# A scan of sixteen steps moved two slots later in a software pipeline of two layers on one core

## The reference, cut to what matters

```python
xn = layernorm(x)                                          # layer 0
s  = (q @ k.T * GAMMA ** (i - j)) @ v                      # retention
h  = silu(tlin(xn, w1)) * tlin(xn, w2)                     # "z"
h  = gelu(tlin(h, h1)); h = gelu(tlin(h, h2))
x  = x + s * silu(tlin(h, w3))
xn = layernorm(x)                                          # layer 1
x_ssm, gate = split(xn @ W_in + b_in)
xc = silu(causal_conv(x_ssm, 4 taps) + conv_b)
B, C = split(xc @ W_x + b_x)
h_t = exp(-exp(A_log)) * h_(t-1) + xc_t[:, None] * B_t     # 128 features x 16 states
y_t = sum over states of C_t * h_t, + D * xc_t
s  = (y * silu(gate)) @ W_out + b_out
x  = x + s * silu(router_ffn(xn))                          # top 512 of 1024 tokens by score
```

## Time and profile before

| what | us |
|---|---|
| median of 3 runs | 546.79 (545.92 to 547.64) |
| the profiled execution | 545.56 |
| its span, first to last instruction | 543.8 |
| busy: PE, DVE, POOL, ACT | 443.4, 407.9, 404.7, 291.4 |

### The profile page before, as it was taken

How to read it: one execution, slowest core, us unless ns; L and a number is a source line. 1 busy time by engine, 2 the same in 40 slices (tenths; PEclk the granted TensorE clock), 3 DMA queues, 4 the chain that set the end, 5 groups by cost and what they waited for, 6 DMA issues and landing times.

```text
span 543.8 us, 6040 instructions
## 1 busy us (share of the span) xinstructions
PE 443.4 (82%) x1777; PEld 259.0 (48%) x1791; DVE 407.9 (75%) x659; ACT 291.4 (54%) x475; POOL 404.7 (74%) x316
## 2 busy tenths in 40 slices
PE   0796978898889897989899888989798999485743
PEld 0575645644564455545565456445554464131211
DVE  2282144959788977989598959898789779958985
ACT  3664736774567545763676366745676447313300
POOL 1673543887599959985999769985999599855582
PEclk9997979899999999999999999999999999978865
DMA  8300006311513143221532162214321332215220
GB/s 316 136 20 4 1 0 175 85 51 40 155 60 86 50 125 108 77 77 47 152 96 78 37 176 77 79 39 118 115 79 58 96 99 78 78 44 165 85 74 19
DMA packets 25379, 46.97 MB, mean 86 GB/s; under 512 B 3072, under 2 KB 4096, under 8 KB 25088
## 3 DMA queue, kind: packets, MB, share of 16 engines
q1 hardware_dynamic: 24336, 45.13, 28.1%
q10 hardware_dynamic: 1008, 1.41, 0.8%
HBM read 42.33 MB, written 4.19 MB: 86 GB/s over the span
## 4 chain that ended last, share of the span: by engine, by line
POOL 35%; DVE 23%; issue 17%; PE 16%; ACT 5%; DMA 1%; SPq 0%; DVEq 0%; POOLq 0%; ACTq 0%
POOL hs L548 15%; DVE hs L1359 10%; PE bank0a L932 7%; DVE xbank L1336 7%; POOL hidAl L510 6%; POOL hidBl L510 5%; PE bank1a L1012 2%; POOL xnTl L492 2%; POOL g L526 2%; POOL g L522 2%; DMA Bt<-w_in 1%; POOL xr L530 1%; POOL q L499 1%; PE ybank L1071 1%; DVE st L1262 1%
## 5 line engine op out<-in xcount | busy, mean ns | idle before, releaser
L548 POOL TENSOR_TENSOR hs<-hs,Ct 128x512 f32<-128x512 f32 x127 | 184.6, 1459 | 32.6 <-DVE hs L1359 19.7
L510 POOL TENSOR_TENSOR hidAl<-plain,hidAh 128x512 fp32r<-128x512 f32 x48 | 64.6, 1346 | 37.7 <-ACT hidAh L643 31.3
L1359 DVE TENSOR_TENSOR_SCAN hs<-decay,carry,xbank 128x512 f32<-128x512 f32 x63 | 80.5, 1278 | 7.6
L510 POOL TENSOR_TENSOR hidBl<-plain,hidBh 128x512 fp32r<-128x512 f32 x48 | 66.1, 1378 | 26.6 <-ACT hidBh L643 18.7
L1359 DVE TENSOR_TENSOR_SCAN hs<-decay,xbank 128x512 f32<-128x512 f32 x64 | 78.0, 1219 | 5.6 <-DVE xbank L1336 0.5
L1336 DVE TENSOR_TENSOR xbank<-xs,bbank 128x512 f32<-128x512 f32 x104 | 71.4, 687 | 1.3
L642 ACT ACTIVATE plain<-bank0a,col 128x512 f32<-128x512 f32 x64 | 44.2, 690 | 45.2 <-PE bank0a L932 44.0
L932 PE MATMUL bank0a<-hidBh,hTh 128*128 128x512 f32 x128 | 57.7, 451 | 1.7 <-ACT q L675 1.7
L932 PE MATMUL bank0a<-hidAh,hTh 128*128 128x512 f32 x128 | 57.0, 445 | 1.7 <-ACT q L675 1.7
L932 PE MATMUL bank0a<-hidAl,hTh 128*128 128x512 f32 x128 | 51.6, 403 | 0.0
L932 PE MATMUL bank0a<-hidBl,hTh 128*128 128x512 f32 x128 | 50.7, 396 | 0.0
(11 more groups left out here) (184 smaller groups left out, 951.7 us busy)
## 6 DMA issues: line engine op xcount, KB each, us to landing
xs<-x_rows SPq DMA_DIRECT2D x128, 256.0 KB, 3.4
xt<-x_tok SPq DMA_DIRECT2D x8, 256.0 KB, 4.5
xr<-x_feat SPq DMA_DIRECT2D x8, 256.0 KB, 7.6
x_rows<-xc SPq DMA_DIRECT2D x8, 256.0 KB, 2.0
out<-xr SPq DMA_DIRECT2D x7, 256.0 KB, 2.2
fh<-h_w SPq DMA_DIRECT2D x1, 1024.0 KB, 10.0
hs<-h_w SPq DMA_DIRECT2D x1, 1024.0 KB, 11.9
lw<-l_w ACTq DMA_DIRECT2D x1, 640.0 KB, 5.4
```

The costliest lines, as they stand in the source:

```text
L510: pool.tensor_tensor(low[:, m, :], plain[:, k % NPLAIN, :], high[:, m, :].bitcast(F32), ALU.subtract).then_inc(hidden_low, 1)
L548: pool.tensor_tensor(h, h, Ct[:, hs_(u)], ALU.mult).then_inc(p_ready, 1)
L1359: dve.tensor_tensor_scan(hs[:, i % NSTATES, :], decay[:, gr:gr + 1].broadcast_to([P, HALF]), xbank[:], 0.0 if u % 2 == 0 else carry[:, k:k ...
```

## The change

`LEAD` goes from 8 to 10: slots 10 to 15 hold steps 0 to 5, and slots 0 to 9 of the next period hold steps 6 to 15. All that belongs to the scan moves with it: DVE's two instructions and POOL's `weigh_states` of each step by two slots, quads 1, 2 and 3 from slots 1, 4, 8 to 3, 6, 10, quad 0 only from 14 to 15, `gate_y` from 9 to 12, ACT's copy of B from 8 to 11. SP's row transfers no longer come as four at once in slot 6; they follow one per slot across the units. The last period has two slots more.

```diff
-LEAD = NGRP // 2
+LEAD = 10
...
-                if n is not None and s == 6:
+                if n == 0 and s == 6:
                     for k in range(NROWS - 1):
-                        spread_x(n, k)
+                        spread_x(0, k)
                 u, k = scanned(p, s)
-                if u is not None and k + NROWS - 1 < NGRP:
-                    spread_x(u, k + NROWS - 1)
+                if u is not None and step(u, k + NROWS - 1) <= LAST:
+                    spread_x(*divmod(step(u, k + NROWS - 1), NGRP))
...
                     elif s == 8:
                         score_columns(n)
-                        keep_B(n)
...
+                if n is not None and s == 11:
+                    keep_B(n)
...
-                    if s in (1, 4) and t is not None:
-                        gather_y(t, 1 if s == 1 else 2)
+                    if s in (3, 6) and t is not None:
+                        gather_y(t, 1 if s == 3 else 2)
...
-                    if s == 8 and t is not None:
+                    if s == 10 and t is not None:
                         gather_y(t, 3)
...
-                    if t == UNITS - 1 and s == 9:
+                    if t == UNITS - 1 and s == 11:
                         project_last()
...
-                    if n is not None and s == 14:
+                    if n is not None and s == 15:
                         gather_y(n, 0)
...
-                    if t == UNITS - 1 and s == 8:
+                    if t == UNITS - 1 and s == 10:
                         finish_last()
-                    elif t < UNITS - 1 and s == 9:
+                    elif t < UNITS - 1 and s == 12:
                         gate_y(t)
```

## The result

| | before | after |
|---|---|---|
| median, us | 546.95 (545.92 to 547.64, 4 runs) | 586.37 (583.48 to 589.67, 4 runs) |
| ratio | | 1.072 (1.066 to 1.079) |
| span of the profiled execution, us | 543.8 | 587.9 |
| mean granted clock | 0.95 | 0.90 |

The change makes the kernel 7.2% slower. The forecast had the sign and half of the size: 20 us where the medians show 39.4. The profiled execution after is the slowest of its four (589.67 us), so what is read from it adds up to 44.1 us of span.

A forecast was written before the change was run, and what follows sets the result against it. POOL's list was taken to bound stretch B (from zero, POOL's first low part of h1 in slot 6, to DVE's residual), a chain through DVE stretch A; 18.0 for six periods + 0.5 + 1.1 = 19.6, giving 567 us, range 552 to 580.

The forecast's parts named there:

- DVE's holes: DVE's idle waits for the new B and the gate's product, 41.8 us; filling them was claimed to give 0.
- SP's queue and B's copy: Row transfers one per slot and ACT's 0.6 us copy in slot 11; claimed value 0 for both.
- Quad 3, slot 8 to slot 10: PE's quad ahead of h2 waits for POOL's step of slot 9; h2 3.3 us later a period, ends 1.7 and 3.8.
- the 3.8 of the upper end: h2's start 3.8 us later, if POOL pays its whole stall before the step of slot 9 instead of beside it.
- The 0.5 that I took off for `rstd`: POOL's 1.02 us `rstd` may run beside the wide comparison in every other period; h2's delay 3.3 instead of 3.8.
- clock mostly kept: Part of the main forecast, chance 0.44: PE waits in slot 10, 3 us a period, its clock mostly not falling.
- the rival given 0.26: PE's clock falls in most periods around the slot 10 wait, 1.8 us more a period, 577 us; chance 0.26.
- Quad 0: Slot 14 to 15, behind `mod_up`, ahead of `ffn_out`: silu starts 0.5 us later a period, slack used up.
- -0.8 for quads 1 and 2: Quad 2 leaves the chain ahead of the convolution, -1.00; quad 1 costs about 0.2; -0.8 a period, ends -1.0 and 0.
- Start and end: Period 0 gets only quad 0's +0.5; the end +4.4 for two more steps, -2.2 and -1.1 for waits, +1.1.
- the signs that the prediction named: Quad 3 waits 2 us or more, h2 some 17 after zero, POOL idle, residual waits 3 or more, period 61 to 63.

The follow-up runs named there:

- experiment 4: Kernel after plus 4 + 2 PE products that nobody reads, ahead of and behind xn's transposes in slot 9; 567.2 us, ratio 1.043.
- experiment 1: Kernel after with quad 3 behind h2's first tile in slot 10 instead of ahead of it; 566.5 us, ratio 1.041.
- experiment 12: Kernel before with quad 2 alone moved from slot 4 to slot 6; 537.6 us, ratio 0.985.
- experiment 11: Kernel before with quad 1 moved to slot 3 and quad 2 to slot 6; 544.5 us, ratio 0.999.
- experiment 6: Kernel after with quad 3 behind h2's first tile, DVE's wide comparison moved from slot 10 to 12, narrow ones one slot later; 568.5 us, ratio 1.038.
- experiment 8: Kernel after with quad 3 behind h2's first tile, wide comparison in slot 12, three unread PE products in slot 9; 562.0 us, ratio 1.029.
- experiment 10: Scan one slot later than before instead of two (`LEAD = 9`), quads 1, 2, 3, 0 in slots 2, 6, 9, 14; 555.4 us, ratio 1.020.
- experiment 9: Kernel of experiment 8 with quad 0 moved back from slot 15 to slot 14; 560.3 us, ratio 1.027.
- experiment 7: Kernel after with the wide comparison moved from slot 10 to 12, narrow ones one slot later, quad 3 still ahead of h2; 588.7 us, ratio 1.079.
- experiment 3: Kernel before plus only a PE wait ahead of h2 in slot 10 until POOL has weighed slot 9's state; 565.4 us, ratio 1.039.

## Why the prediction was wrong

The direction and the place were right, the size of the main terms was not. The forecast was 19.6 us of growth; the medians show 39.4 and the profiled execution 44.1.

- **Right: DVE's holes are worth nothing.** They closed, and 41.8 us of waiting came back as 47.2 elsewhere. SP's queue and B's copy cost next to nothing: their only waits of any length, one of 9.8 us and one of 3.1 us, stand in period 0, where DVE had waited 9.5 us before as well.
- **Failed: the term "Quad 3, slot 8 to slot 10", 3.3 us a period.** With the clock kept (experiment 4) h2 starts 4.5 us later on average and the six stretches B grow by 26.8 us, quad 0's share included. In period 2 of the kernel after h2 came 5.46 us late (19.42 - 13.96): 3.8 + 0.81 + 0.87, which are the 3.8 of the upper end; 0.81 because the step came 17.55 after zero, not 16.74; 0.87 because the quad ran at half clock. The 0.5 that I took off for `rstd` running beside the comparison was wrong in sign: `rstd` 1.46 instead of 1.02 and the last low part 1.73 instead of 1.27 lie beside DVE's products with B in SBUF and a narrow comparison, which now come earlier. The stall of 2.04 us is there in full, but ahead of `rstd`.
- **A reading that failed with it:** I had h2 wait for h1's last low part. The earlier trace rows say ACT's `q`, behind xn and `rstd`, and that path is 1.9 us late after the change (experiment 1). So PE waits 4.92 us for xn first, and then 1.78 for the step, where I had one wait of 3.3.
- **Failed: "clock mostly kept".** This was the rival given 0.26, and it too was too small, 1.8 us a period and nothing in stretch A. I counted PE's wait ahead of the quad, not what quad 3 did by standing in slot 8. Half clock cost 0.87 in the quad and 1.3 in h2's first tile in period 2, and in the six stretches B 13.3 us, 2.2 a period (the kernel after against experiment 4). Stretch A lost 4.8 us by it (the window at 260). By the ratios experiment 4 gave back 16 us in all. TensorE: Matmul & The Clock Gate (the Trainium skill, Part 1) has it that idleness brings the throttle back; the rows agree with 0.50 behind 4.9 us without work. Why the clock was also kept some 40 us later, in stretch A, is not shown; the products of slot 9 aren't the reason, since experiment 1 keeps it there without them.
- **Quad 0: +0.5 forecast, +0.19 measured** (`mod_up` to silu 9.52 instead of 9.33). Right in kind: the third `mod_up` waits 0.84 for ACT; the slack and a tighter `ffn_out` take up most of it.
- **"-0.8 for quads 1 and 2": right with the clock kept, failed with it fallen.** Where the clock stays, as in most stretches of experiments 1 and 4, stretch A is 24.1 and 25.0 in turn instead of 25.0 and 26.1, 0.9 to 1.0 less. That is quad 2's -1.2 (experiment 12) and quad 1's +0.3 where I had -1.0 and +0.2. Where the clock falls, quad 1 costs 1.7 (experiment 11). Together the five stretches A gained nothing: +1.7 us instead of -4.
- **Start and end: +0.5 and +1.1 forecast, -0.8 and +0.5 measured,** once the 2.7 us ahead of the first zero are left out.

Of the signs that the prediction named, h2's start (17 us or more after zero), POOL's idle time ahead of h2's low parts and DVE's two closed holes came. The quad's wait (1.78 us in period 2, not 2 or more), the residual's wait (2.31, not 3) and the period (64.7 us on average, not 61 to 63) lay outside what it gave.

The same split for the other kernels, as the profiled executions show it, in us against the kernel before:

| kernel | ahead of the first zero | to period 1's zero | six stretches B | five stretches A | end | sum |
|---|---|---|---|---|---|---|
| after | +2.7 | -0.8 | +40.1 | +1.7 | +0.5 | +44.1 |
| experiment 1 | -0.4 | -2.3 | +27.1 | -3.2 | -0.2 | +21.0 |
| experiment 4 | -0.6 | -2.3 | +26.8 | -3.2 | +0.4 | +21.1 |
| experiment 6 | +0.6 | +1.9 | +20.2 | -1.5 | +2.4 | +23.6 |
| experiment 8 | +2.4 | +1.3 | +12.4 | -1.5 | +2.9 | +17.5 |
| experiment 10 | -0.8 | -1.4 | +16.9 | -6.0 | -1.5 | +7.2 |
| experiment 12 | +2.0 | -1.2 | +0.3 | -6.0 | -1.5 | -6.4 |

By cause, each from its own run: the wait for the step ahead of h2 about 17 us (experiment 1, with the part of the clock that goes with it), the half clock 16 (experiment 4; the two overlap), and 15 to 17 us remain in both kernels in which h2 is on time and the clock kept (experiments 8 and 9). Of these, 11 to 12 us are stretch B, about 2 a period: mostly quad 3's own 1.0 and its wait of 0.5 to 0.7 on PE behind h2's start, where there is no slack. The rest lies at the start and the end; part of it was there before the first instruction that differs, and what the moved comparison does to it is open.

## What to carry to other kernels

Filling the idle time of an engine that isn't the bound gave nothing here; moving its work moved other engines' waits, and these decided. Before a small product is moved, look at what it does where it stands: a quad that waits in an idle stretch can be what keeps the clock up, and one that doesn't wait may stand in a chain for nothing, as quad 2 did, the one piece of this change that was worth making alone (1.5%). A stall of one engine beside another's wide instruction was not lost by rescheduling; ask onto which instruction it falls next, and who awaits that one. And read in the rows which wait ends last: h2 hung on ACT's `q`, not on the low part that the code names beside it.

## What the runs showed of the hardware

- A POOL instruction of 128 x 512 took 3.31 to 3.35 us beside DVE's comparison of 2048 columns, 1.7 to 1.8 beside DVE's products with B in SBUF or a narrow comparison, and about 1.27 otherwise. Moving the comparison left 2.0 to 2.1 us of stall on whatever instruction stood beside it (4.54 us for two in experiment 7).
- DVE pays too: the product with B in SBUF takes 1.75 to 1.80 us beside POOL's work in the kernel after, 0.68 with B in PSUM.
- One idle stretch of PE of 2.9 to 4.9 us around slot 9 (the kernel after and experiments 1, 3, 6 and 10) was followed by a granted clock of 0.50. In period 2 of the kernel after this lasted 10 us, from 222 to 232. In slot 1 of experiment 11 one stretch of 2.29 us was followed by it and one of 2.13 was not. Two stretches of 1.28 and 0.91 us, with a quad and the retention's products between them, were not.
- Products that nobody reads can pay: 36 of them gave back 16 us of 586.
